# A graph network on one core: forty-eight waves of gathers for forty-seven, seven tiles fetched row by row for thirteen, and eight column numbers a wave in the weighing

## The reference

```python
x = _layernorm(x + _L0_gnn_ref(x, edge_index, edge_type_4, ...))   # 4 steps
x = _layernorm(x + _L1_gnn_ref(x, edge_index, edge_attr_2, ...))
x = _layernorm(x + _L2_gnn_ref(x, edge_index, edge_type_9, ...))
x = _layernorm(x + _L3_gnn_ref(x, edge_index, edge_attr_10, ...))

# L0, one of four steps: a row of a table for every edge, summed by dst, then a GRU
m = (embedding @ W_msg.T + b_msg).reshape(n, 4, 128)
r = segment_sum(m[src, etype], dst, num_segments=n)
embedding = _gru_cell(r, embedding, w_ih, w_hh, b_ih, b_hh)

# L1: the message is a product with an edge term; mean by dst
msg = pe * x[src] + x[src]          # pe = relu(edge_w @ pos_w1) @ pos_w2
agg = segment_sum(msg, dst) / maximum(segment_sum(1, dst), 1)

# L2: as L0, once, with an embedding of the edge type added

# L3: attention with 8 heads of 16
ex = exp(alpha - amax[dst])
alpha = ex / (segment_sum(ex, dst) + 1e-16)
out = segment_sum((v[src] + e) * alpha, dst)
```

## Time and profile before

| | |
|---|---|
| median of 3 runs | 4213.75 us (4209.95 to 4215.1) |
| the profiled execution | 4215.39 us, of which the profile's span is 4213.5 us |
| granted TensorE clock, mean | 0.822 of full |
| GpSimd busy | 2686.4 us (64%) |
| TensorE matmul busy | 2810.1 us (67%) |
| VectorE busy | 1824.5 us (43%) |
| ScalarE busy | 924.9 us (22%) |
| DMA packets under 512 B | 60775 of 161997 |

### The profile page before, as it was taken

How to read it: one execution, slowest core, us unless ns; L and a number is a source line. 1 busy time by engine, 2 the same in 40 slices (tenths; PEclk the granted TensorE clock), 3 DMA queues, 4 the chain that set the end, 5 groups by cost and what they waited for, 6 DMA issues and landing times. The chain is left out here.

```text
span 4213.5 us, 69693 instructions
## 1 busy us (share of the span) xinstructions
PE 2810.1 (67%) x12039; PEld 2106.2 (50%) x12040; DVE 1824.5 (43%) x4894; ACT 924.9 (22%) x3024; POOL 2686.4 (64%) x2809
## 2 busy tenths in 40 slices
PE   6666685556855658656677877776657766664697
PEld 3444444444444444444456766644445555564584
DVE  5222252222522226444463333422223766666985
ACT  2111231111311113111123322321112111111233
POOL 3777767777677776777727777367775377775000
PEclk8777797777977779787879999977778888887799
DMA  6222222222222222222212222022221254553240
GB/s 172 55 55 55 55 89 55 55 55 54 90 55 55 55 54 90 55 55 55 54 43 55 54 53 54 22 55 55 55 55 42 75 159 152 154 157 112 100 160 16
DMA packets 161997, 310.42 MB, mean 74 GB/s; under 512 B 60775, under 2 KB 84654, under 8 KB 161218
## 3 DMA queue, kind: packets, MB, share of 16 engines
q0 software_dynamic: 92704, 203.66, 18.1%
q1 hardware_dynamic: 62626, 102.68, 7.4%
q10 hardware_dynamic: 6400, 1.65, 0.2%
HBM read 246.12 MB, written 61.65 MB: 73 GB/s over the span
## 5 line engine op out<-in xcount | busy, mean ns | idle before, releaser
L743 POOL DMA_INDIRECT ring<-m_tab,idx x1504 | 1434.4, 954 | 537.5 <-issue 498.8
L1824 PE MATMUL ps<-oh,ring 128*128 128x256 f32 (+1 forms) x2816 | 886.9, 476 | 501.2 <-DMA ring<-m_tab,idx 304.1
L1824 PE MATMUL ps<-nodes,ring 128*128 128x256 f32 (+1 forms) x2624 | 798.8, 464 | 415.0 <-DMA ring<-m_tab,idx 235.8
L869 ACT ACTIVATE ring<-ring 128x128 f32 x2256 | 486.9, 295 | 2148.9 <-DMA ring<-m_tab,idx 893.7
L1824 PEld LDWEIGHTS ps<-oh,ring 128*128 128x128 f32 x2816 | 626.9, 247 | 662.1 <-issue 562.6
L743 POOL DMA_INDIRECT ring<-x_tab,idx x752 | 714.1, 950 | 238.4 <-issue 227.0
L1824 PEld LDWEIGHTS ps<-nodes,ring 128*128 128x128 f32 x2624 | 567.9, 241 | 557.8 <-issue 467.8
L1260 DVE TENSOR_SCALAR oh<-iota,dl 128x256 f32<-128x256 f32 x1200 | 371.5, 380 | 959.4 <-PE ps L1824 959.0
L1260 DVE TENSOR_SCALAR nodes<-iota,dl 128x256 f32<-128x256 f32 x1194 | 368.1, 378 | 713.4 <-PE ps L1824 713.4
L743 POOL DMA_INDIRECT ring<-kv_tab,idx x416 | 406.5, 977 | 134.7 <-issue 126.5
L1824 PE MATMUL ps<-wpad,rts 128*128 128x128 f32 x832 | 164.8, 379 | 191.2 <-DVE pw L1565 191.2
(11 more groups left out here) (290 smaller groups left out, 2759.1 us busy)
## 6 DMA issues: line engine op xcount, KB each, us to landing
nodes<-m_tab SPq DMA_DIRECT2D x4096, 0.5 KB
rec<-m_tab ACTq DMA_DIRECT2D x2560, 0.5 KB
nodes<-x_tab SPq DMA_DIRECT2D x2048, 0.5 KB
ve_dr<-pw SPq DMA_DIRECT2D x52, 512.0 KB, 3.0
ring<-ve_dr SPq DMA_DIRECT2D x52, 512.0 KB, 3.4
ring<-m_tab,idx POOLq DMA_INDIRECT x1504, 2.5
m_tab<-ring SPq DMA_DIRECT2D x75, 256.0 KB, 2.2
ring<-x_tab,idx POOLq DMA_INDIRECT x752, 2.5
```

What stands on the lines that cost most here:

```text
L743: pool.indirect_dma_start(rows[:, j, :], None, table, bass.IndirectOffsetOnAxis(ap=idx[:, wave * WV + j:wave * WV + j + 1], axis=0)).then_ ...
L869: ins = nc.scalar.activation(ring_flat[:, ds(r[j], P)], rows[:, j, :], ACT.Copy)
L1824: return T.matmul(o, lhsT, rhs, start=start, stop=stop, skip_group_check=True)
```

## The change

FULL becomes 48, so GpSimd gathers 48 waves (384 tiles) in each of passes 0 to 5, and 7 tiles are far ones: 4 for SyncE, 3 for ScalarE, none for GpSimd. ScalarE issues 9 rows behind a wave. In pass 4 GpSimd fetches ScalarE's 3, behind wave 39. The last waves are taken in the order 44, 48 (far), 45, 46, 47, 49, 50. ScalarE waits for the row numbers behind the copies of wave 0 of a pass, ahead of its first row. In the weighing TensorE's sequencer loads eight numbers a wave from `cols` with `load_cols`. Denominators now lie 32 f32 columns apart, 128 bytes, so the number of a window's first column, taken as a byte address in a view of `ps` as bytes, is also that of its denominators. The steps on `cols_b` go.

```diff
+DEN_W = P // 4
-FULL = 47
+FULL = 48
 NEAR = FULL * WV
 FAR = TILES - NEAR
-SP_TILES, ACT_TILES = 8, 5
-POOL_FAR = FAR - SP_TILES - ACT_TILES
-ACT_ROWS = 15
+SP_TILES, ACT_TILES = 4, 3
+ACT_ROWS = 9
...
-            if t1 > SP_TILES + ACT_TILES:
-                eng.wait_ge(x_pl, (k + 1) * (16 * POOL_FAR))
...
-        TAIL_WAVES = (FULL - 3, FULL, FULL - 2, FULL + 1, FULL - 1, M_WAVES, M_WAVES + 1)
+        TAIL_WAVES = (FULL - 4, FULL, FULL - 3, FULL - 2, FULL - 1, M_WAVES, M_WAVES + 1)
...
-                    if not single(k) and g == FULL // 2:
-                        for t in range(SP_TILES + ACT_TILES, FAR):
-                            far_gather(table, idx, t, x_pl)
                     if k == PASS_L1 and g == FULL - 9:
                         for t in range(SP_TILES, SP_TILES + ACT_TILES):
                             far_gather(table, idx, t, x_l1)
...
                         keep(r, j, wave_rows(g, p % DEPTH), j == n - 1)
+                    if p == 0:
+                        act.wait_ge(xi_ld, 64)
                     act_rows(table, j0, p * ACT_ROWS)
 
             act.wait_ge(s_dv, DV["x_ka"])
             act.wait_ge(s_pe, PE["dT"])
-            act.wait_ge(xi_ld, 64)
...
-            step("b_cv", V.tensor_copy(cols_v, cols[:, :].rearrange("p (g j) -> p g j", j=WV)))
-            step("b_c8", V.tensor_scalar(cols_d, ...))
-            after("b_c8")
-            step("b_c24", V.tensor_scalar(cols_d, cols_d, 3, NP, ALU.mult, ALU.add))
...
-            parts = psf[:, NP:NP + WIN * 24].rearrange("p (w k h) -> p w h k", k=3, h=HEADS)
+            parts = psf[:, NP:NP + WIN * DEN_W].rearrange("p (w x) -> p w x", x=DEN_W)[:, :, 0:24].rearrange(
+                "p w (k h) -> p w h k", h=HEADS)
...
+            den_at = psf[:, NP:NP + WIN * DEN_W].bitcast(U8)
+
             def weigh(t, par, last):
                 for u in range(RING):
-                    cs = load_both(pe, cols_b, t * RING + u)
+                    cs = load_cols(pe, cols, t, u)
                     if u == 0:
                         pe.wait_ge(b_e2, t + 1)
                     pe.wait_ge(b_ohb, t * RING + (u + 1))
                     for j in range(WV):
-                        mm(psf[:, ds(cs[WV + j], 24)], ohb[:, u, j, :], ex3f[:, par, u * WV + j, :], start=False,
+                        mm(den_at[:, ds(cs[j], 96)].bitcast(F32), ohb[:, u, j, :], ex3f[:, par, u * WV + j, :], start=False,
                            stop=False)
```

More of the change, by code:

```diff
@@ L47 @@
 M_FIRST = 5
-FULL = 47
+DEN_W = P // 4
+FULL = 48
 NEAR = FULL * WV
 FAR = TILES - NEAR
-SP_TILES, ACT_TILES = 8, 5
-POOL_FAR = FAR - SP_TILES - ACT_TILES
-ACT_ROWS = 15
+SP_TILES, ACT_TILES = 4, 3
+assert SP_TILES + ACT_TILES == FAR
+ACT_ROWS = 9
 ROW = 4 * D
@@ L106, in load_rows @@
         skip_runtime_bounds_check_because="the row numbers that the gathers use, below the table's length")[1]
[L109 to L113, removed]
 def load_tiles(eng, tix, i, which=mybir.EngineType.DVE, n=WV):
@@ L210, in build @@
         basef = cols_b[:, 0:SLOTS].bitcast(F32)
-        cols_v, cols_d = (cols_b[:, :].rearrange("p (g k j) -> p g k j", k=2, j=WV)[:, :, k, :] for k in range(2))
         ring = sb("ring", [P, RING, WV, 2 * D])
@@ L301, in build @@
         x_l1 = sem("x_l1")
-        x_pl = sem("x_pl")
         x_sp = [sem(f"x_sp{i}") for i in range(4)]
@@ L1529, in _ @@
             dve.wait_ge(ln_x, 3 * NCH)
-            step("b_cv", V.tensor_copy(cols_v, cols[:, :].rearrange("p (g j) -> p g j", j=WV)))
-            step("b_c8", V.tensor_scalar(cols_d, cols[:, :].rearrange("p (g j) -> p g j", j=WV), 4, None,
-                                         ALU.arith_shift_right))
-            after("b_c8")
-            step("b_c24", V.tensor_scalar(cols_d, cols_d, 3, NP, ALU.mult, ALU.add))
             def one_hot_of(u, wave):
```

## The result

The changed kernel takes 4219.89 us (median of 20 runs, 4214.23 to 4231.02) and the kernel before 4216.56 us (20 runs, 4209.95 to 4220.59). The ratio is 1.0013, with a 95% interval of 1.0007 to 1.0019: 5.5 us slower (3 to 8), inside the 0.2% that the prediction counts as no change. The two medians lie only 3.3 us apart; the ratio is used from here on. The forecast was no change, 4215 us within 4204 to 4226.

A forecast was written before the change was run, and what follows sets the result against it. GpSimd's gathers, mostly idle for "issue", were taken to bound most passes, TensorE's sequencer the weighing. The terms +30.0 + 4.2 - 6.3 - 3.3 - 23.5 gave +1.1 us: 4215 us, range 4204 to 4226.

The forecast's parts named there:

- Gathers, +30.0: Passes 0, 1, 2 and 5: six more GpSimd gathers each, all on the path, 7.5 us a pass, +30.0 us.
- The rival of hidden gathers: Passes 0, 1, 2, 5: TensorE's tail ends them, so the 30.0 us vanish and the kernel takes 4185; chance 0.04.
- Weighing, -23.5: Weighing of L3: TensorE's sequencer loads eight column numbers for sixteen, waves shorten; -23.5 us, bounds -26.8 to -13.3.
- all of the 0.515 us should come off: Weighing: the sequencer's sum is the wave, so the load's whole saving shortens each; 49 x 0.515 = 25.2 us.
- The slower rival: Weighing: VectorE or another engine takes over, only the visible idle time, -13.3 us, comes back; 4225 us, chance 0.17.
- Start, -3.3: Start of pass 0: the moved ScalarE wait gives back TensorE's 3.26 us of idle time; -3.3 us, bounds 0 and -11.3.
- Pass 3, +4.2: End of pass 3: last three tiles come 7.5 us later, TensorE finishes 3.6 to 4.8 us later; +4.2 us taken.
- The upper case of +4.8: Pass 3: if TensorE is as late by itself as now, it finishes 4.8 us later.
- Pass 4, -6.3: Pass 4: wave 44 can start earlier with fewer extra gathers before it; -6.3 us, bounds -8.8 to +5.0.

The follow-up runs named there:

- the shares alone: Kernel before with only the new shares of tiles, far gathers and order of last waves: 4227.26 us, ratio 1.0029, 12.2 us slower.
- the longer load: Kernel before with the changed kernel's byte addresses of denominators, sixteen numbers still loaded a wave: 5991.9 us on a slow chip, ratio 1.0027.
- without the division: Changed kernel with the denominators' addresses made without a division, from column numbers divided once by VectorE: 4205.69 us, ratio 0.9985 to the kernel before.
- The moved wait alone: Kernel before with only ScalarE's wait for the row numbers moved behind wave 0's copies: 4211.27 us, ratio 0.9994.
- the store just as short and the old shares: Kernel before with one row-number table first, wait moved, pass 4's far gathers later, and division-free weighing of eight numbers: 4179.62 us, ratio 0.9916.
- the weighing alone: Kernel before with only the weighing's part of the change (eight numbers a wave, denominators 32 columns apart, byte addresses): 4207.77 us, ratio 0.9983.

## Why the prediction was right, and where it was not

**Right as a time, by luck: its errors cancelled.** The forecast of +1.1 us stands beside +5.5 (3 to 8) measured. The term of the weighing was wrong by 19 us, and the start, pass 3 and pass 4 gave most of that back.

**Gathers, +30.0: right in passes 1, 2 and 5.** There they cost 6.9, 7.0 and 7.6 us in the changed kernel, and 6.6 to 7.2 with the shares alone. Pass 0 has them too, but its start gave back more. The rival of hidden gathers is out: the passes do end with the last gather. Row queues that had less to do gave nothing back within the passes that the traces could tell. The rule of the Trainium skill (page Perfetto Trace Analysis, section GPSIMD Engine Instruction) to go by spacing and not by spans holds: six gathers by the spans of 0.952 us would be 5.7 us a pass.

**Weighing, -23.5: wrong.** It gave -4.8. The step that failed is "all of the 0.515 us should come off". The load did shorten by that, and where the sequencer is the limit it is worth 26 us. But the sum of the sequencer took the addresses as unchanged, by the order of instructions, in which one instruction stands for one. What that instruction holds had changed: a division and an addition more, 416 times. That costs 13.7 us in the changed kernel (166.6 to 152.9) and 21.1 us with the longer load. The other 5 us of the miss are a limit that the prediction put too low: without the division a wave takes 2.90 us and not 2.78, since the 128-column matmuls then follow each other without a gap and still take 1.88 us. The slower rival pointed the right way (it had the stage at -13.3) with a wrong mechanism: VectorE was not what held the changed kernel's wave at 3.17 us, since with the division gone it falls to 2.90.

**Start, -3.3: right for the move by itself, not for the change.** The moved wait alone gives 3.5 us. The changed kernel gave 7.0 on GpSimd's wait, the same start in the kernel without the division 9.9, and the shares alone 9.9 without the move. What the prediction left out is that fewer far tiles mean fewer row numbers to store: they come soon enough that ScalarE's wait stops nobody, wherever it stands. That accounts for TensorE's 3.26 us of idle time, not for the rest. With the store just as short and the old shares the wait is 10.80 us. The rest has two parts that the traces show. First, TensorE starts sooner: at 68.4 to 69.6 us in the kernels with seven far tiles and at 69.9 to 72.4 in those with fifteen. By its program it waits there for VectorE's copies of what it transposed last (`t_d1`, L2021), and it starts 1.0 to 1.1 us behind the first of them in all seven. That copy starts 0.1 us after the transposes end with seven far tiles, and 1.3 to 3.2 us after it with fifteen, as in the kernel before:

```profile
69.97 0.56 DVE L1398 COPY pw<-ps 128x384 f32<-128x384 f32 x1 [4.36 <-remote]
```

Second, the granted clock: with fifteen far tiles it is 0.66 to 0.83 from 70 to 80 us, with seven it is 1.00. What makes the copy late, and whether the clock follows from it, stays open.

**Pass 3, +4.2: too high.** The start-to-start difference is +0.4 in the changed kernel and +1.9 with the shares alone. By the means of the four fast-chip kernels with the old pass (554.4) and the three with the new one (556.2) it is +1.9. TensorE is indeed no longer late: VectorE's wait for it ends 1.9 us after the last three tiles in all three, for 5.7 to 7.0. What was mis-sized is how much later these tiles come, counted from the pass's first gather: some 6 us and not 7.5. In the old kernels GpSimd waits 1.5 to 1.8 us for TensorE in this pass, where the prediction had no wait at all, and in the new ones it doesn't. (The upper case of +4.8 can't be redone from the rows; the 1.0 us between transfer and first matmul gives +4.5.)

**Pass 4, -6.3: right, and a clock on top.** VectorE's last step is at 498.7, 503.3 and 501.2 us in the three kernels with the new shares, and at 506.0, 509.2 and 510.8 in those with the old: 7.6 us on average. The rest of the 13.0 us comes behind it. These are slices of the work after pass 4 (us, busy times, granted clock, DMA share, GB/s), in the kernel before:

```profile
2740.00:2750.00 10.00, 9.79 (x33) 7.38 (x34) 3.94 (x8) 1.30 (x4) 2.02 (x2) 0.50 0.09 26
```

and in the changed kernel, as far behind the end of the pass:

```profile
2746.00:2756.00 10.00, 8.68 (x53) 5.93 (x52) 5.87 (x12) 3.27 (x6) 3.02 (x3) 1.00 0.17 52
```

At the same place in the work TensorE has 0.50 of its clock (1.2 GHz) in the one and all of it (2.4 GHz) in the other, and the chain of small matmuls there takes 51.5 us for 47.4. Two kernels whose pass 4 is as before, the moved wait alone and the weighing alone, show 51.3 and 47.4, so this is not the change's. It would also account for 4 of the 4.4 us by which the two profiled executions stand closer (1.1 us) than the ratio says (5.5 us); no trace shows how often the other executions have it.

**Added up with these runs:** start and pass 0 together some -3 (-0.9, -4.0 and -4.4 in the three kernels with the new shares), passes 1, 2 and 5 +21, pass 3 +2, pass 4 -8, weighing -5, thus about +7, inside the measured 3 to 8.

## What to carry to other kernels

A row of an order that stands for one instruction before and one after can hold different arithmetic: where an address is computed at run time, read what is computed, and keep divisions out of it, since in a stage that the sequencer paces they are paid in full. Look for the next limit as well: here TensorE's own matmuls kept 5 us of the gain. When a share of work moves between engines, its preparation moves too (tables of row numbers, their stores and loads), and it may lie on the path where the work itself does not. A sum that comes out right tells nothing of its terms: check each by its own stretch of the trace, and by more than one trace where the effect is a few microseconds.

## What the runs showed of the hardware

A division and an addition in TensorE's sequencer cost 51 ns a matmul here where it was the limit (21.1 us over 416). One cheap register operation more in each of the sixteen addresses of a wave made the time from the first 24-column matmul to the first 128-column one 1.00 us for 0.94. Loading eight column numbers took 592 ns and sixteen 1107. On two chips every kernel, the one before too, took about 42% longer, while the old weighing, which has no gathers, kept its 171.2 us; the mean time between gathers in the passes was 1.8 us for 1.26.
